# Source lists of 34 relations in a graph kernel: which matmul operand carries the one-hot, and where the lists are turned

## The reference, cut to what matters

```python
seg  = edge_type_34 * n + dst
agg  = segment_sum(h[src], seg, 34 * n)
mean = agg / max(cnt, 1)
h1   = einsum('nri,rio->no', mean, W_rel) + h @ W_root + b
```

## Time and profile before

| | us |
|---|---|
| median of 3 runs | 2396.64 |
| lowest and highest run | 2394.74, 2404.66 |
| profiled execution | 2400.8 |
| its span in the trace | 2399.0 |
| PE busy | 2065.2 |
| DVE busy | 1118.9 |
| ACT busy | 722.4 |
| POOL busy | 556.2 |

### The profile page before, as it was taken

The page is one execution under the profiler, slowest core; times in us unless marked ns, Lnnn a source line. Parts: engine busy times, 40 slices in busy tenths (PEclk is TensorE's granted clock), DMA queues, the critical chain, the costliest instruction groups (busy, mean ns, idle before and its releaser), DMA issues.

```text
span 2399.0 us, 33918 instructions
## 1 busy us (share of the span) xinstructions
PE 2065.2 (86%) x10740; PEld 1728.6 (72%) x10741; DVE 1118.9 (47%) x2046; ACT 722.4 (30%) x944; POOL 556.2 (23%) x538
## 2 busy tenths in 40 slices
PE   3999789989999999689999999967989768767885
PEld 3999787558789985389989999964556746647663
DVE  5752122234343652435555555532233776656773
ACT  1222121012212210035545554531010256312763
POOL 0000765630000046324444453104620000000000
PEclk8999899999999999889999999988999889885998
DMA  3556456844446458548878777857840021110111
GB/s 108 156 157 185 137 152 210 267 151 130 138 148 188 154 175 268 173 130 264 262 255 261 251 259 250 267 194 238 268 156 8 0 68 28 53 31 26 53 50 38
DMA packets 203264, 378.31 MB, mean 158 GB/s; under 512 B 18810, under 2 KB 173626, under 8 KB 203176
## 3 DMA queue, kind: packets, MB, share of 16 engines
q1 hardware_dynamic: 170520, 246.23, 31.7%
q0 software_dynamic: 31216, 128.89, 17.6%
q10 hardware_dynamic: 1440, 1.97, 0.2%
HBM read 288.68 MB, written 88.34 MB: 157 GB/s over the span
## 4 chain that ended last, share of the span: by engine, by line
PE 74%; DVE 10%; issue 6%; DMA 4%; ACT 4%; ACTq 0%; another core or an unknown queue 0%; SPq 0%; DVEq 0%; POOL 0%; POOLq 0%
PE ps L1575 41%; PE ps L1483 14%; PE ps L1773 5%; PE ps L1738 2%; DMA arena<-in_L_gnn_W_rel 2%; PE ps L1588 2%; PE ps L1701 1%; PE ps L1809 1%; ACT arena L731 1%; PE ps L1468 1%; PE ps L1466 1%; PE ps L1824 1%; PE ps L1427 1%; DVE counts L899 1%; DVE arena L1240 1%
## 5 line engine op out<-in xcount | busy, mean ns | idle before, releaser
L1575 PE MATMUL ps<-w_hi,hT_hi 128*128 128x384 f32 x2172 | 766.0, 353 | 62.3 <-issue 25.6
L1575 PE MATMUL ps<-w_hi,hT_lo 128*128 128x384 f32 x2172 | 738.5, 340 | 0.8 <-issue 0.8
L1575 PE MATMUL ps<-w_lo,hT_hi 128*128 128x384 f32 x2172 | 738.3, 340 | 0.0
L1575 PEld LDWEIGHTS ps<-w_hi,hT_hi 128*128 128x128 f32 x2172 | 418.1, 193 | 75.0 <-issue 54.4
L1575 PEld LDWEIGHTS ps<-w_lo,hT_hi 128*128 128x128 f32 x2172 | 418.2, 193 | 0.2
L1575 PEld LDWEIGHTS ps<-w_hi,hT_lo 128*128 128x128 f32 x2172 | 416.7, 192 | 1.0 <-issue 0.9
L478 POOL DMA_INDIRECT arena<-U,ix x252 | 252.6, 1002 | 521.5 <-DVE ov L1000 355.0
L1483 PE MATMUL ps<-arena,onehot 128*128 128x512 f32 x1008 | 336.6, 493 | 32.2 <-issue 19.7
L1483 PEld LDWEIGHTS ps<-arena,onehot 128*128 128x128 f32 x1008 | 189.8, 191 | 179.6 <-issue 167.7
L1040 DVE TENSOR_TENSOR w_lo<-arena,w_hi 128x2304 fp32r<-128x2304 f32 x67 | 171.4, 2558 | 139.0 <-ACT w_hi L609 131.3
L558 ACT ACTIVATE arena<-ps 128x384 f32<-128x384 f32 x160 | 78.3, 491 | 494.5 <-PE ps L1575 449.1
(11 more groups left out here) (238 smaller groups left out, 2179.4 us busy)
## 6 DMA issues: line engine op xcount, KB each, us to landing
arena<-in_L_gnn_W_rel SPq DMA_DIRECT2D x74, 1152.0 KB, 5.6
U<-arena SPq DMA_DIRECT2D x292, 192.0 KB
arena<-in_L_gnn_W SPq DMA_DIRECT2D x36, 1152.0 KB
U<-z SPq DMA_DIRECT2D x28, 864.0 KB
arena<-rows_d SPq DMA_DIRECT2D x42, 320.0 KB, 3.4
arena<-in_L_gnn_root SPq DMA_DIRECT2D x4, 1152.0 KB
arena<-U,ix POOLq DMA_INDIRECT x252
arena<-in_L_gnn_W_root SPq DMA_DIRECT2D x2, 1152.0 KB
```

The costliest lines, as they stand in the source:

```text
L1575: ins = pe.matmul(acc, l, r[:, j, kt, :], start=(n == 0), stop=(n == 3 * KT - 1))
```

## The change

`node_list` swaps the operands. The one-hot (128 x 256, fp16) is now the moving operand, and the stationary one is a slice of 34 columns of `nidz`, a strip of 67 columns per group with the node numbers in the middle column and zeros around it. The slice is shifted so that the node numbers stand in column r. Five matmuls of 256 columns make a list, and it lands in row r of `ps[0:34, 7, 0:256]`; the other rows get zeros added. The lists are then rows, and have to be turned: DVE copies them into `has`, PE transposes them in two pieces (`lists_turned()`), DVE copies the result into `lidx`. `lists_turned()` stands in PE's queue after the five steps of the root's half j = 0. On DVE the copy, the wait for the transposes and the copy into `lidx` all stand where the one copy stood. `nidz` is filled by DVE ahead of the first list; it lies in `oh_s`, which is free then. The counts in `further()` rise by one.

```diff
+        nidz = oh_s[:].rearrange("p b n -> p (b n)")[:, 0:NG * (2 * R1 - 1)].rearrange("p (g n) -> p g n", g=NG)
...
             def list_one_hot(r, b):
 
+                if r == 0:
+                    dve.wait_ge(S["c_pe"], NT + 2)
+                    link(dve.memset(nidz, 0.0))
+                    dve.tensor_copy(nidz[:, :, R1 - 1:R1], nid[:].unsqueeze(2))
                 dve.wait_ge(S["l_pe"], r + 1)
...
-                    dve.wait_ge(S["l_pe"], R1 + c + 3)
+                    dve.wait_ge(S["l_pe"], R1 + c + 4)
...
                     dve.wait_ge(S["l_pe"], R1 + 2)
-                    dve.tensor_copy(lidx[:], ps[:, 7, 0:TC * R1]).then_inc(S["l_ix"], 1)
+                    dve.tensor_copy(has[:, 0:TC * P], ps[0:R1, 7, 0:TC * P]).then_inc(S["l_oh"], 1)
+                    dve.wait_ge(S["l_pe"], R1 + 3)
+                    dve.tensor_copy(lidx[:].rearrange("p (r k) -> p k r", k=TC),
+                                    ps[:, 7, TC * P:TC * (P + R1)].rearrange("p (k r) -> p k r", k=TC)).then_inc(S["l_ix"], 1)
...
                 for j in range(2):
                     for g in range(NG):
                         step(0, o + 2 * nr + j, g)
+                    if side and j == 0:
+                        lists_turned()
...
             def node_list(r, b):
 
                 pe.wait_ge(S["l_oh"], r + 1)
+                for g in range(NG):
+                    ins = pe.matmul(ps[0:R1, 7, 0:TC * P], nidz[:, g, R1 - 1 - r:2 * R1 - 1 - r], oh_l[:, b, g, :],
+                                    start=False, stop=True, skip_group_check=True)
+                ins.then_inc(S["l_pe"], 1)
+
+            def lists_turned():
+
+                pe.wait_ge(S["l_oh"], R1 + 1)
                 for k in range(TC):
-                    for g in range(NG):
-                        ins = pe.matmul(ps[:, 7, TC * r + k:TC * r + k + 1], oh_l[:, b, g, P * k:P * (k + 1)], nid[:, g:g + 1],
-                                        start=False, stop=True, skip_group_check=True)
+                    ins = pe.transpose(ps[:, 7, TC * P + R1 * k:TC * P + R1 * (k + 1)], has[:, P * k:P * (k + 1)], ident[0:R1, 0:R1])
                 ins.then_inc(S["l_pe"], 1)
...
-                    pe.wait_ge(S["l_oh"], R1 + c + 1)
+                    pe.wait_ge(S["l_oh"], R1 + c + 2)
```

## The result

The changed kernel takes 2419.3 us (median of 4 runs) against 2395.7 beside it: 1.0106 times as long, with a 95% interval of 1.0081 to 1.0131. The forecast of 2414.6 in 2406 to 2427 holds. Which terms of its sum hold is another matter, and the three stages tell. The first fence has stretches of the changed kernel: the lists, from the root's start to the first messages, and the messages; the columns are those of the earlier trace rows.

The account below looks back on a forecast made before the run. PE was taken as the bound in the lists, with DVE's and POOL's queues between lists and messages. 8.2 + 6.6 + 1.5 + 1.7 = 18.0 us took the median from 2396.6 to 2414.6, range 2406 to 2427.

Parts of the forecast that it names:

- Part 1, the lists: PE's list stretch: five matmuls of 256 columns per list instead of ten of one column, +8.2 us, bounds +7.7 and +10.5.
- 18.8 + 0.5 for the 20 changes of type: PE's lists: 18.8 us to stream 170 matmuls and 0.5 for changes of operand type, 19.3 where lists cost 11.1 before.
- the 81 to 84 us given as a sign of being right: The length that the list stretch on PE would have if the forecast was right; it was 73.5 us before.
- the 0.8 of the rival: PE's lists: a single list at over 0.8 us would show exposed loads and the forecast wrong; about 0.55 was expected.
- The odd start column: Rival on PE's lists: loads of the shifted slices are exposed, 17 us on top, 2432; chance 0.08.
- Part 2, DVE ahead of the lists: DVE's memset and copy before the first one-hots take 0.3 to 0.8 us, covered by 1.7 us of slack: nothing added.
- Part 3, the turn: DVE's queue in the root: its wait for the transposes delays split, `further_list` and bias additions; messages at E' + 41.8, +6.6 us.
- Part 4, POOL: The first gather ahead of the messages, held by DVE's additions, makes PE wait 0 to 2.7 us; middle taken, +1.5.
- the three cases: POOL's first gather is ready at E' + 37.3, 39.4 or 41.4, depending on whether it slips between DVE's three additions.
- Part 5, the clock: After PE's pause ahead of the messages the clock falls to the 1.2 GHz level: +1.7 us, bounds 0 and 3.4.
- the tail was not hidden: Denies the rival that the turn in the root is free and only the lists cost: +8.2, 2405; chance 0.04.
- the messages kept their pauses: Denies the rival that PE's 8.0 us of pauses in the messages go: +6.3, 2403, not slower; chance 0.05.

Follow-up runs that it names:

- wide_128: The changed kernel with stationary slices of 128 columns instead of 34, output on 128 partitions; 1.0072 times the kernel before.
- w128_late: The changed kernel with slices of 128 columns and the wait and copy into `lidx` moved behind `further_list()`; 1.0032 times the kernel before.
- tail_free: The kernel before with the late wait, DVE meant to be held after `further_list` until POOL passed its first gather, but hardly held; single run, 2371.0 us.
- tail_only: The kernel before, lists unchanged, with DVE's copy of the lists waiting for PE's five steps of root half j = 0; 1.0064 times the kernel before.
- turn_late: The changed kernel with the wait for the transposes and the copy into `lidx` moved behind `further_list()` on DVE; 1.0052 times the kernel before.
- wide_64: The changed kernel with stationary slices of 64 columns instead of 34; single run, 2396.5 us.

## Why the prediction was right, and where it was not

*Part 1, the lists: the wrong size.* +8.2 was forecast, with +10.5 as the upper end; it was +13.6. The streaming was right: ten matmuls last 1.27 us with a last one of 0.273, so 0.111 each, for 0.110 forecast. (The Trainium skill, "TensorE: Matmul & The Clock Gate", section "Back-to-back issue gap", gives 131 ns for 512 columns in a stream and 81 for 128, from which 98 ns for 256 is an estimate; the row disagrees here too. Its formula for a single gap, N/2.4 + 2.5, gives 109 ns, and with that the trace agrees.)

The step that failed is "I take 18.8 + 0.5 for the 20 changes of type". The 0.5 came from the earlier trace rows, where the stationary side has 128 columns; the changes here are of width too, and measured 87.1 less 62.4 and 18.9, 5.8 us over 20, 0.29 each. wide_128 shows that all but 0.02 of it is the width, and its list stretch of 81.7 is the forecast 8.2 over the 73.5 of before. The same 0.02, for the same change of types, tells that the upper bound was reasoned wrongly too: it took the 0.14 us a step that the lists cost before, beside their matmuls, for a price of the change of types. What those 0.14 are, no run shows.

The sentence "That sum takes the loading of the 34 stationary columns as hidden" fell with it in part: the loads inside a list are hidden, the first of a list and the first behind it are not. Each takes 0.10 us, as in the earlier trace rows, and not the 0.028 of the prediction's estimate. The earlier trace rows could not tell, for its load has the same width as the matmul ahead. The rows beside it in that timeline could have: the load for L1468 at 691.23, shown above, waits. The list stretch missed the 81 to 84 us given as a sign of being right, while a list, at 0.65 us with its first load, stayed below the 0.8 of the rival. The odd start column, that rival with 0.08, had no part: wide_128 and w128_late have odd starts as well.

*Part 2, DVE ahead of the lists: right.* Memset and copy took from 768.13 to 768.6; no list waited by more than the 0.2 us that one of them did.

*Part 3, the turn: right.* DVE's wait, PE's pause (2.79 for 3.0), the order of what is late next, all came as worked out. With the gather out of the way (tail_free) the messages begin at 41.7 for 41.8 forecast. tail_only and turn_late show the cause from both sides: put in alone it costs its 9 us, taken out alone it gives them back. The turn itself is nearly free.

*Part 4, POOL: right in kind, small in size.* Of the three cases, the held gather came: +3.0 at 44.8, against the middle value of 1.5 and an upper end of 2.7. Landing took 3.25 us after its end, for 3.1. It was no chance of one run: in all four with the late wait and DVE not held (the changed kernel, tail_only, wide_128, wide_64) the gather takes 7.15 or 7.16 us and the messages begin at 44.4 to 44.8.

*Part 5, the clock: near in size, its condition not settled.* Behind PE's pause of 2.79 us the granted clock is 0.5 for three microseconds, and at the start of the messages for four. The fence has the changed kernel's stretches of 1 us, columns as in the earlier trace rows; for the clock, the row of 874 stands for three and the row of 900 for four.

```profile
873.00:874.00 1.00, 0.38 (x1) 0.38 (x2) 0.96 (x3) 0.14 (x1) 0.00 (x0) 0.83 0.00 0
874.00:875.00 1.00, 1.00 (x4) 1.00 (x4) 1.00 (x1) 0.00 (x0) 0.00 (x0) 0.50 0.39 23
...
877.00:878.00 1.00, 1.00 (x7) 1.00 (x6) 1.00 (x1) 0.00 (x0) 0.00 (x0) 0.96 1.07 404
```

```profile
900.00:901.00 1.00, 1.00 (x2) 0.40 (x2) 0.00 (x0) 0.00 (x0) 0.70 (x2) 0.50 0.98 381
...
904.00:905.00 1.00, 1.00 (x4) 0.71 (x3) 0.03 (x1) 0.00 (x0) 0.85 (x1) 0.81 0.72 295
```

The engine is at the 1.2 GHz level from 899.57 to about 904.4, 4.8 us, 2.4 lost where 1.7 was forecast. On the other chips the same is seen where the gather was late: in wide_64, tail_only and wide_128 the clock is at that level for 2.9, 3.4 and 5.8 us of the messages (from their stretches of 1 us), and they are 1.5, 2.0 and 2.9 longer than 108.7. In tail_free the gather came in time, PE waited 3.19 us ahead of the messages, and the clock stayed at 1.00 all through them; they are 1.3 longer all the same, 0.4 of it idle time of PE. So with the messages at 41.7, next to the 41.8 of part 3, nothing of the forecast 1.7 came. Where the clock did fall at their start, the gather was late and PE's wait ahead of them was 4.7 to 7.6 us. The length of the pause alone doesn't sort the cases: 2.79 us were followed by a fall in the root, 3.19 us here by none.

*The sum.* 18.0 was forecast; the stages show 26.4 and the medians 23.6, and the time came out 4.7 over the 2414.6 (from a base of 2395.7, where the forecast had 2396.6). That the range held is partly luck. Both the lists (13.6 for at most 10.5) and the gather (3.0 for at most 2.7) went over their bounds, and the stages' 26.4 is over the 23.2 of all high ends together; the median came out 2.8 under the stages, just below the 2420 that the high ends gave. With 26.4 on top of 2396.6, 2423, it would have held only by the widening to 2427, whose reason, loads that are exposed in part, is what came. No rival came: the tail was not hidden, and the messages kept their pauses.

## What to carry to other kernels

Before a narrow stationary operand is put between wide ones, look in the timeline at the load behind the switch, not at a load inside a run of equal ones; padding the narrow side with zeros to the width of its neighbours was worth 5.4 us at 20 places here, and some 17 us in the counting stage, which the change had not touched. A wait that a new helper needs belongs behind all work on its engine that others wait for; moving one copy behind `further_list()` took the stretch from 44.8 back to 35.7 us. And price an operand swap by the columns it streams: ten matmuls of one column were cheaper than five of 256.

## What the runs showed of the hardware that was not expected

- A change of the number of stationary columns, 34 or 64 to 128 and back, cost PE 0.27 us (34) and 0.29 us (64) per visit to the narrow width in the lists, beside what is streamed, and 0.20 us in the counting stage, while a change between fp16 and f32r at 128 columns cost 0.02. Why was not seen; what the traces show is that the load at a change of width starts late: 0.15 us after the start of a matmul that streams 128 columns, where without the change of width it starts together with that matmul.
- An indirect gather of POOL that begins under one of DVE's long two-input additions ended 0.82 to 0.83 us after one of them: after the first of three in one run (3.20 us in all), after the second of two in the kernel before (5.09), after the third of three in four runs (7.15 or 7.16). Which one it will be, nothing here tells.
- The same kernel lost 8.0 us in one stage of messages on one chip, in pauses of about 1 us, and 0.04 us on another.
